# Five token-shift mixes of a recurrent stage on VectorE alone, its 64-row products in pairs, its row norms on ScalarE

## The chip, the cores and the metric

The kernel runs on one core of a Trainium2 chip. It has five engines that run their own instruction streams and meet at semaphores: TensorE (PE in the profile) for matrix products, VectorE (DVE), ScalarE (ACT), GpSimd (POOL) and SyncE (SP), which issues most transfers. The time is device microseconds of one execution of the whole program, as the median of several runs.

## What is computed

The reference is a chain of four blocks over 16 sequences of 128 rows of 512 numbers, in float32: attention over the rows and then over a context with an MLP, a grouped cross attention, a recurrent block, and a latent attention with an MLP. Only the third is touched. It is

```python
xa = _ln(x, ln1_w, ln1_b)
sx = jnp.concatenate([state[:, 1:2] - xa[:, :1], xa[:, :-1] - xa[:, 1:]], axis=1)
xxx = jnp.tanh((xa + sx * maa_x) @ maa_w1).reshape(b, l, 5, DM)
xxx = jnp.einsum('blfd,fde->blfe', xxx, maa_w2)
xm = xa[:, :, None] + sx[:, :, None] * (maa_stack + xxx)
xk, xw, xv, xr, xg = (xm[:, :, j] for j in range(5))
w = jnp.exp(-jnp.exp(time_decay + jnp.tanh(xw @ td_w1) @ td_w2))
# r, k, v = xr @ Wr.T, xk @ Wk.T, xv @ Wv.T;  g = silu(xg @ Wg.T)
def step(s, rkvw):
    a = k_t[..., :, None] * v_t[..., None, :]
    out = jnp.einsum('bhi,bhij->bhj', r_t, u * a + s)
    return a + w_t[..., :, None] * s, out
# out is normed per head, gated by g, projected by Wo, added to x, normed again,
# shifted with the row before and sent through a gated feed-forward layer
```

The five rows of `xm` are the mixes: each is the normed row plus the difference to the row before it, times a factor that comes from a product of rank 32.

## The kernel before

The recurrent stage is `recurrence_phase`. Every engine runs the same pipeline of steps (`run_steps`, line 2142). In one step five sequences are in work at five depths: `ahead` is being loaded and normed, `front` is mixed and projected, `middle` is scanned, `back` is normed by heads and projected, `tail` leaves the feed-forward layer. With 16 sequences there are 20 steps, of which twelve have all five. The order of work inside a step is written out by hand, once for each engine, in that engine's own `step` function, and an engine never goes past an instruction that waits.

- VectorE: for the middle sequence, eight units u of `inputs(u)` (the product of keys and values, line 2665) and `scan(u)` (the decaying sum, line 2677), with everything else put between them. `mix` (line 2651) multiplies a bank of the factor by the row difference `sx_t` into the tile `mixtmp`, one instruction for each of the five mixes, in the order 1, 2, 0, 3, 4. `norm_apply` (line 2630) scales the rows of `ahead` and `back`. `make_gate` (line 2656) and `shift_front` (line 2643, which makes `sx_t`) stand at the end of a step.
- GpSimd: `multiply_states` (line 2396) multiplies each scan's result by the receptance; `add_rows` (line 2389) adds the rows `xa_t` to `mixtmp` into one of two tiles `xm`; `rsqrt` (line 2378) raises a variance to the power -1/2; `bonus_values` is line 2403.
- TensorE: `low_rank` (line 2903) forms the first rank-32 product with features on the partitions, in a piece of 128 rows and one of 32. `mix_pair` (line 2915) and `mix` (line 2930) form the factors with 64-row weights; `mix_pair` alternates two of them, which lie in different halves of the rows. `decay_high` (line 2947) has the same 64-row form. `project`, `keys` (line 2876), `rows` (line 2882) and the transposes (line 2869) follow. `sum_heads` (line 2984) adds up each unit after GpSimd's product.
- ScalarE: `low_rank_tanh` (line 2501, five pieces), `first_states` (line 2466, the first column that a scan needs), `make_decay` (line 2472), `rows_front` (line 2481, scales and shifts the transposed rows into `xa_t`), `gate` (line 2535).

Products go through five PSUM banks, a to d and n. `StepBanks` holds a list of which item uses which bank in what order; TensorE fills a bank (`begin`, `done`), and whoever reads it last gives it back.

## Time and profile before

| | |
|---|---|
| median of three runs | 3513.13 us (3513.01 to 3519.1) |
| profiled execution | 3515.94 us |
| its span, first to last instruction | 3514.2 us |
| mean granted TensorE clock of the span | 0.975 of full speed |
| busy over the span: PE, DVE, ACT, POOL | 3222.5, 1748.5, 1131.0, 900.5 us |

The recurrent stage lies from about 1571 to 2516 us of the span. A step of the steady part is seen best in the order of time of each engine. A row of that view gives the start, the busy time, the engine and line, what is written and read with shapes, how many alike stand in a row, and in brackets how long the engine had stood idle before it and who ended the idleness. A scan has the name `TENSOR_TENSOR_SCAN` in the trace and `SCALAR_TENSOR_TENSOR` in the tables of the order.

### The profile page before, as it was taken

The page shows a single profiled execution, that of the slowest core. Times are in us where ns is not written, and L with a number is a line of the kernel's source. Part 1 is how long each engine was busy: PE and PEld are TensorE (multiplying, and loading weights), DVE is VectorE, ACT ScalarE, POOL GpSimd, SP SyncE. Part 2 cuts the span into 40 slices and gives each one's busy share as a digit, 9 for nine tenths or more (in the row PEclk, how much of TensorE's full clock was granted, in tenths as well). Part 3 has the DMA queues.
Part 4 walks back from the last instruction along what each step waited for, and adds up shares of the span by engine and source line. Part 5 has one row for each costly group of instructions (what it writes and reads, how often), then busy time and mean ns, then how long its engine had stood idle before and what let it go on. Part 6 is the DMA issues. An engine that isn't in the chain of part 4 may idle for free. (4 is left out here: it accounts for less than half of the span.)

```text
span 3514.2 us, 52783 instructions
## 1 busy us (share of the span) xinstructions
PE 3222.5 (92%) x19344; PEld 2128.6 (61%) x19344; DVE 1748.5 (50%) x2503; ACT 1131.0 (32%) x4052; POOL 900.5 (26%) x614
## 2 busy tenths in 40 slices
PE   7999899989999888867899999997799999899999
PEld 5665556557666555546666666664455555466675
DVE  4555556510000378864788888888264454400000
ACT  2444234412111366642232332332133333311111
POOL 2333233300000022223555555565100000100000
PEclk9999999999999899988999999999899999999999
DMA  4110321110000141111011111110130110101010
GB/s 164 43 41 32 119 89 56 34 66 12 24 15 21 40 159 48 44 62 40 26 46 37 36 49 37 36 46 28 60 128 32 33 41 22 49 19 36 21 33 12
DMA packets 104308, 170.19 MB, mean 48 GB/s; under 512 B 16512, under 2 KB 54016, under 8 KB 100736
## 3 DMA queue, kind: packets, MB, share of 16 engines
q1 hardware_dynamic: 99296, 124.58, 11.1%
q10 hardware_dynamic: 4896, 44.04, 3.1%
q8 instruction: 75, 1.23, 0.1%
q14 instruction: 41, 0.34, 0.0%
HBM read 135.03 MB, written 33.55 MB: 48 GB/s over the span
## 5 line engine op out<-in xcount | busy, mean ns | idle before, releaser
L2396 POOL TENSOR_TENSOR rec_S<-rec_S,rec_r_t 128x1024 f32<-128x1024 f32 x128 | 309.8, 2421 | 315.1 <-DVE rec_S L2677 315.1
L2677 DVE TENSOR_TENSOR_SCAN rec_S<-rec_decay,rec_S 128x1024 f32<-128x1024 f32 x128 | 321.9, 2515 | 22.7 <-ACT rec_S L2466 19.4
L2076 PE MATMUL mlp_bank<-mlp_src_t,region_a 128*128 128x256 f32 x1024 | 224.8, 382 | 3.1 <-ACT mlp_src_t L1997 3.1
L2076 PE MATMUL pmlp_bank<-pmlp_src_t,region_a 128*128 128x256 f32 x1024 | 224.9, 382 | 1.9 <-ACT pmlp_src_t L1997 1.9
L2088 PE MATMUL mlp_bank<-region_a,mlp_h_t 128*128 128x512 f32 x512 | 221.1, 592 | 0.0
L2088 PE MATMUL pmlp_bank<-region_a,pmlp_h_t 128*128 128x512 f32 x512 | 221.1, 592 | 0.0
L2076 PEld LDWEIGHTS mlp_bank<-mlp_src_t,region_a 128*128 128x128 f32 x1024 | 196.5, 192 | 33.3 <-issue 6.8
L2076 PEld LDWEIGHTS pmlp_bank<-pmlp_src_t,region_a 128*128 128x128 f32 x1024 | 196.5, 192 | 32.0 <-issue 5.5
L1505 ACT ACTIVATE group_scores<-group_scores,group_negmax 128x128 f32<-128x128 f32 x512 | 197.6, 391 | 28.6 <-DVE group_negmax L1599 18.7
L2043 DVE TENSOR_TENSOR mlp_y<-mlp_bank,mlp_xres 128x512 f32<-128x512 f32 x16 | 11.1, 691 | 375.4 <-PE mlp_bank L2088 375.4
L2043 DVE TENSOR_TENSOR pmlp_y<-pmlp_bank,pmlp_xres 128x512 f32<-128x512 f32 x16 | 11.1, 691 | 364.6 <-PE pmlp_bank L2088 364.6
L2088 PEld LDWEIGHTS mlp_bank<-region_a,mlp_h_t 128*128 128x128 f32 x512 | 96.9, 190 | 118.5 <-issue 118.5
L2088 PEld LDWEIGHTS pmlp_bank<-region_a,pmlp_h_t 128*128 128x128 f32 x512 | 96.9, 190 | 118.5 <-issue 118.5
L2006 ACT ACTIVATE pmlp_h_t<-pmlp_bank,vectors 128x256 f32<-128x256 f32 x128 | 53.7, 470 | 353.8 <-PE pmlp_bank L2076 353.8
L2006 ACT ACTIVATE mlp_h_t<-mlp_bank,vectors 128x256 f32<-128x256 f32 x128 | 53.7, 470 | 348.6 <-PE mlp_bank L2076 348.6
L2665 DVE TENSOR_TENSOR rec_S<-rec_vb,rec_k 128x1016 f32<-128x1016 f32 x128 | 154.0, 1203 | 0.0
L599 ACT ACTIVATE latent_scores<-latent_scores,region_a 128x256 f32<-128x256 f32 x256 | 126.4, 497 | 71.6 <-DVE region_a L789 71.6
L2984 PE MATMUL rec_rec_out<-rec_S,head_sum 128*32 128x256 f32 x1024 | 86.4, 400 | 57.6 <-POOL rec_S L2396 57.6
L973 PE MATMUL latent_pjA<-latent_src_t,F_query_key 128*128 128x512 f32 x256 | 122.0, 602 | 3.3 <-ACT latent_k_t L589 2.3
L599 ACT ACTIVATE self_scores<-self_scores,self_negmax 128x128 f32<-128x128 f32 x256 | 98.8, 391 | 77.1 <-DVE self_negmax L789 77.1
L599 ACT ACTIVATE cross_scores<-cross_scores,cross_negmax 128x128 f32<-128x128 f32 x256 | 98.8, 390 | 76.4 <-DVE cross_negmax L789 76.4
L2389 POOL TENSOR_TENSOR rec_xm<-rec_mixtmp,rec_xa_t 128x512 f32<-128x512 f32 x80 | 106.8, 1335 | 64.2 <-DVE rec_mixtmp L2651 64.2
(363 smaller groups left out, 6496.4 us busy)
## 6 DMA issues: line engine op xcount, KB each, us to landing
rec_vb<-v_by_head SPq DMA_DIRECT2D x32, 512.0 KB, 4.2
region_a<-in_C_w ACTq DMA_DIRECT2D x2, 4096.0 KB, 20.5
region_a<-in_G_w ACTq DMA_DIRECT2D x2, 4096.0 KB, 19.5
self_xres<-in_x SPq DMA_DIRECT2D x16, 256.0 KB, 2.6
rows_A<-self_xres SPq DMA_DIRECT2D x16, 256.0 KB, 2.0
cross_ctx_t<-in_ctx_t SPq DMA_DIRECT2D x16, 256.0 KB, 3.3
cross_xres<-rows_A SPq DMA_DIRECT2D x16, 256.0 KB, 2.6
rows_B<-cross_xres SPq DMA_DIRECT2D x16, 256.0 KB, 2.0
```

What stands on the lines that cost most here:

```text
L599: nc.scalar.activation(S[:, u, at, :], S[:, u, at, :], ACT.Exp, bias=negmax[:, u, at.start // KB:at.start // KB + 1], accum_out=rowsum[:, ...
L973: last = nc.tensor.matmul(pj.bank(item)[:, :], Wk[:, c, n * 128:n * 128 + 128], src_t[:, c, :, :], start=c == 0, stop=c == C - 1)
L1505: nc.scalar.activation(S[:, u, at, :], S[:, u, at, :], ACT.Exp, bias=negmax[:, u, at:at + 1], accum_out=rowsum[:, u // UPS, sum_column(u, ...
L2006: hidden = nc.scalar.activation(h_t[:, 2 * n + i, :], ph.bank(("h", n))[:, i * TT:(i + 1) * TT], ACT.Gelu_apprx_tanh, bias=vec(cfg["b1"], ...
L2043: nc.vector.tensor_tensor(y[:, k, :], po.bank(("out", k))[:, :], xres[:, k, :], ALU.add)\
L2076: product = nc.tensor.matmul(ph.bank(item)[:, i * TT:(i + 1) * TT], W1[:, c, f:f + 128], src_t[:, c, :, :], start=c == 0, stop=c == C - 1)
L2088: product = nc.tensor.matmul(po.bank(item)[:, :], h_t[:, c, k * T:k * T + T], W2[:, c, :], start=c == 0, stop=c == HC - 1)
L2389: nc.gpsimd.tensor_tensor(xm[at % 2][:, :, :], mixtmp[:, :, :], xa_t[:, :, 1:T + 1], ALU.add)\
L2396: nc.gpsimd.tensor_tensor(S[u % 4][:, :, :], S[u % 4][:, :, :], bcast(r_t[:, s.k, UNITS[u][0], :], [128, JH, T], 1), ALU.mult)\
L2665: nc.vector.tensor_tensor(S[u % 4][:, :, 1:T], vb[jh][:, :, 0:T - 1], bcast(k_bank[s.k][:, m * T:m * T + T - 1], [128, JH, T - 1], 1), ALU ...
L2677: nc.vector.tensor_tensor_scan(St[:, :, :].rearrange(flat), decay[m][:, :, :].rearrange(flat), St[:, :, :].rearrange(flat), 0.0, ALU.mult, ...
L2984: last = nc.tensor.matmul(rec_out[32 * g:32 * g + 32, jh * 2 * T:(jh + 1) * 2 * T], head_sum, S[u % 4][:, 2 * g:2 * g + 2, :], start=m == ...
```

## The change

It has four parts, all in the recurrent stage.

1. **The low-rank product** is made with rows on the partitions, all five factors side by side (160 columns). One tanh writes it to `low_rows`, in which a column of ones stands beside each factor. Three transposes bring it to a bank, item `lt`, and ScalarE copies that to the three `low` tiles.
2. **Pairs.** Mixes 1 and 2 lie in one tile now; the decay's second product goes with mix 0 (`decay_and_mix`), mix 3 with mix 4. The halves of output and feed-forward products are split or put together anew around them, and TensorE transposes the rows of `ahead` ahead of the feed-forward keys.
3. **The mixes.** VectorE multiplies in place in the bank, waits for that, and adds the rows from the bank into `xm`. GpSimd's `add_rows` and the tile `mixtmp` are gone. `sx_t` is made from `xa_t` and a copy of it that ScalarE writes back into the bank `x`. `make_gate` moves ahead of the last unit.
4. **The norms.** GpSimd also multiplies the negative mean (formed by VectorE) by the factor, and ScalarE normalises in one instruction with scale and bias.

```diff
-    MIX_TILE = {0: (0, 0), 1: (0, 64), 2: (1, 0), 3: (1, 64), 4: (2, 0)}
+    MIX_TILE = {1: (0, 0), 2: (0, 64), 0: (1, 0), 3: (1, 64), 4: (2, 0)}
...
+        low_rows = sb("low_rows", [128, NMIX, 2 * DM])
-        mixtmp = sb("mixtmp", [128, C, T])
...
-            ("a", "mx", 0), ("b", "mix1", 0), ("a", "mix2", 0), ("n", "mean", 2),
+            ("a", "mx", 0), ("a", "lt", 0), ("b", "mix1", 0), ("a", "mix2", 0), ("n", "mean", 2),
...  GpSimd
+                pool.wait_ge(out_done, n * 2 + 1)
+                nc.gpsimd.tensor_tensor(out[:, 1:2], tile[:, 8:9], out[:, 0:1], ALU.mult).then_inc(out_done, 1)
-            def add_rows(s, f):
-                nc.gpsimd.tensor_tensor(xm[at % 2][:, :, :], mixtmp[:, :, :], xa_t[:, :, 1:T + 1], ALU.add)\
...  ScalarE
+                last.then_inc(first_done, 1)
+                act.wait_ge(first_done, s.n * 3 + 2)
+                nc.scalar.activation(chunks(banks.bank("x")), xa_t[:, :, 1:T + 1], ACT.Copy).then_inc(first_done, 1)
+            def normalise(n, out, rows, scale, scale_done, out_done):
+                act.wait_ge(scale_done, n * 2 + 2)
+                nc.scalar.activation(out[:, :], rows[:, :], ACT.Identity, scale=scale[:, 0:1], bias=scale[:, 1:2])\
+                    .then_inc(out_done, 1)
...
+                nc.scalar.activation(low_rows[:, :, 0:DM],
+                                     banks.bank("mx")[:, 0:NMIX * DM].rearrange("p (f d) -> p f d", f=NMIX), ACT.Tanh)\
+                    .then_inc(banks.free_sem("mx"), 1)
+            def low_rank_copy(s):
+                full(act, s, "lt")
+                for tile in range(3):
+                    p = 128 if tile < 2 else 64
+                    last = nc.scalar.copy(low[tile][0:p, :], banks.bank("lt")[0:p, tile * T:(tile + 1) * T])
+                    last.then_inc(low_done if tile < 2 else banks.free_sem("lt"), 1)
...  VectorE
+                nc.vector.tensor_scalar(tile[:, 8:9], tile[:, 6:7], -1.0, None, ALU.mult)
...
-                nc.vector.tensor_tensor(sx_t[:, :, :], xa_t[:, :, 0:T], xa_t[:, :, 1:T + 1], ALU.subtract)\
-                    .then_inc(sx_done, 1)
+                nc.vector.tensor_tensor(sx_t[:, :, :], xa_t[:, :, 0:T], chunks(banks.bank("x")), ALU.subtract)\
+                    .then_inc(banks.free_sem("x"), 1)
...
-                nc.vector.tensor_tensor(mixtmp[:, :, :], chunks(banks.bank(f"mix{f}")), sx_t[:, :, :], ALU.mult)\
+                bank = chunks(banks.bank(f"mix{f}"))
+                nc.vector.tensor_tensor(bank, bank, sx_t[:, :, :], ALU.mult).then_inc(mixed, 1)
+                dve.wait_ge(mixed, s.n * NMIX + at + 1)
+                nc.vector.tensor_tensor(xm[at % 2][:, :, :], bank, xa_t[:, :, 1:T + 1], ALU.add)\
                     .then_inc(banks.free_sem(f"mix{f}"), 1)
...  TensorE
+                for n, (w, c, t) in enumerate(parts):
+                    last = nc.tensor.matmul(banks.bank("mx")[:, 0:NMIX * DM], xa_t[:, c, t:t + T], w[:, c, :],
+                                            start=n == 0, stop=n == len(parts) - 1)
```

On TensorE the start of a step, from the low-rank product to the first pair, reads before (each row of a matrix product is twice as many passes in the trace):

```order
L2903 MATMUL rec_bank_a<-rec_xa_t,region_a 128x128 x4
L2903 MATMUL rec_bank_a<-rec_xa_t,rec_w_shift 128x128 x4
L2903 MATMUL rec_bank_a<-rec_xa_t,region_a 32x128 x4
L2903 MATMUL rec_bank_a<-rec_xa_t,rec_w_shift 32x128 x4
L2984 MATMUL rec_rec_out<-rec_S,head_sum 32x256 x4
L2915 MATMUL rec_bank_b<-rec_low,region_a 128x128
L2915 MATMUL rec_bank_a<-rec_low,region_a 128x128
```

and now

```order
L2898 MATMUL rec_bank_a<-region_a,rec_xa_t 128x160 x4
L2898 MATMUL rec_bank_a<-rec_w_shift,rec_xa_t 128x160 x4
L2987 MATMUL rec_rec_out<-rec_S,head_sum 32x256 x4
L2906 MATMUL rec_bank_a<-ident,rec_low_rows 128x128 x2
L2906 MATMUL rec_bank_a<-ident,rec_low_rows 64x128
L2880 MATMUL rec_bank_c<-region_a,rec_f_in 128x512
L2913 MATMUL rec_bank_b<-rec_low,region_a 128x128
L2913 MATMUL rec_bank_a<-rec_low,region_a 128x128
```

The four groups of the low-rank product have become two, and the transposes (line 2906) and a quarter of the feed-forward gate stand between it and the pair.

On VectorE, from the first scan of a step to the second mix, before (line 2688 gathers the heads of `back`, line 2692 takes their mean off):

```order
L2677 SCALAR_TENSOR_TENSOR rec_S<-rec_decay,rec_S 128x1024
L2651 TENSOR_TENSOR rec_mixtmp<-rec_bank_b,rec_sx_t 128x512
L2688 TENSOR_TENSOR rec_og<-rec_rec_out,rec_bv 128x512
L2665 TENSOR_TENSOR rec_S<-rec_vb,rec_k 128x8x127
L2692 TENSOR_TENSOR rec_og<-rec_og,rec_bank_n 128x512
L2677 SCALAR_TENSOR_TENSOR rec_S<-rec_decay,rec_S 128x1024
L2651 TENSOR_TENSOR rec_mixtmp<-rec_bank_a,rec_sx_t 128x512
```

and now

```order
L2686 SCALAR_TENSOR_TENSOR rec_S<-rec_decay,rec_S 128x1024
L2652 TENSOR_TENSOR rec_bank_b<-rec_bank_b,rec_sx_t 128x512
L2660 TENSOR_TENSOR rec_xm<-rec_bank_b,rec_xa_t 128x512
L2697 TENSOR_TENSOR rec_og<-rec_rec_out,rec_bv 128x512
L2674 TENSOR_TENSOR rec_S<-rec_vb,rec_k 128x8x127
L2701 TENSOR_TENSOR rec_og<-rec_og,rec_bank_n 128x512
L2686 SCALAR_TENSOR_TENSOR rec_S<-rec_decay,rec_S 128x1024
L2652 TENSOR_TENSOR rec_bank_a<-rec_bank_a,rec_sx_t 128x512
L2660 TENSOR_TENSOR rec_xm<-rec_bank_a,rec_xa_t 128x512
```

Behind each multiplication an addition stands. At the end of the step, from the scan of unit 6 on, VectorE had

```order
L2677 SCALAR_TENSOR_TENSOR rec_S<-rec_decay,rec_S 128x1024
L2630 TENSOR_SCALAR rec_x<-rec_x,rec_stats,rec_rstd 128x512
L2745 SCALAR_TENSOR_TENSOR rec_f_in<-rec_bank_c,rec_w_same,rec_f_in 128x128 x4
L2665 TENSOR_TENSOR rec_S<-rec_vb,rec_k 128x8x127
L2677 SCALAR_TENSOR_TENSOR rec_S<-rec_decay,rec_S 128x1024
L2643 TENSOR_TENSOR rec_sx_t<-rec_xa_t 128x512
L2656 SCALAR_TENSOR_TENSOR rec_g<-rec_g,rec_bank_a 128x512
```

and has

```order
L2686 SCALAR_TENSOR_TENSOR rec_S<-rec_decay,rec_S 128x1024
L2750 SCALAR_TENSOR_TENSOR rec_f_in<-rec_bank_c,rec_w_same,rec_f_in 128x128 x4
L2665 SCALAR_TENSOR_TENSOR rec_g<-rec_g,rec_bank_a 128x512
L2674 TENSOR_TENSOR rec_S<-rec_vb,rec_k 128x8x127
L2686 SCALAR_TENSOR_TENSOR rec_S<-rec_decay,rec_S 128x1024
L2642 TENSOR_TENSOR rec_sx_t<-rec_xa_t,rec_bank_b 128x512
```

The normalisation of `ahead` is gone and the gate (line 2656, now 2665) stands ahead of the last unit.

ScalarE has, from the receptance's copy to the first column of the last unit, before

```order
L2466 COPY rec_S<-rec_s 128x8
L2519 ACTIVATE rec_r_t<-rec_bank_d 128x512
L2492 ACTIVATE rec_f_in<-rec_bank_c,vectors,rec_w_shift 128x127 x8
L2466 COPY rec_S<-rec_s 128x8
L2472 ACTIVATE rec_decay<-rec_e_t 128x8x127
L2541 COPY rec_c_sb<-rec_bank_b 128x128
L2478 COPY rec_xa_t<-rec_st 128x4
L2481 ACTIVATE rec_xa_t<-rec_bank_b,vectors 128x128 x4
L2466 COPY rec_S<-rec_s 128x8
```

and now

```order
L2472 ACTIVATE rec_y<-rec_x,rec_rstd 128x512
L2520 ACTIVATE rec_r_t<-rec_bank_d 128x512
L2489 ACTIVATE rec_f_in<-rec_bank_c,vectors,rec_w_shift 128x127 x8
L2446 COPY rec_S<-rec_s 128x8
L2452 ACTIVATE rec_decay<-rec_e_t 128x8x127
L2472 ACTIVATE rec_x<-rec_x,rec_rstd 128x512
L2536 ACTIVATE rec_g<-rec_bank_a 128x512
L2542 COPY rec_c_sb<-rec_bank_b 128x128
L2460 COPY rec_xa_t<-rec_st 128x4
L2463 ACTIVATE rec_xa_t<-rec_bank_b,vectors 128x128 x4
L2468 ACTIVATE rec_bank_b<-rec_xa_t 128x512
L2446 COPY rec_S<-rec_s 128x8
```

The two normalisations (line 2472), the gate's tanh (line 2536, which stood near the end of the step) and the copy back into the bank (line 2468) have been put into that stretch.

## Rows read from the trace of the kernel before

**Rows 1.** Windows, steady steps: stretch, its us, then the engines' busy us.
```profile
1750.00:2300.00 550.00, 503.60 (x3769) 377.28 (x3767) 474.65 (x614) 174.66 (x470) 311.20 (x195) 1.00 0.13 40
```

**Rows 2.** Waits, 1750 to 2300 us: who waited for whom: us, times, longest.
```profile
DVE rec_mixtmp L2651 <- PE rec_bank_b L2915: 32.5, 10, 3.3
```

**Rows 3.** Timeline of VectorE, one steady step: start us, us, instruction [idle before].
```profile
1990.87 2.29 DVE L2677 TENSOR_TENSOR_SCAN rec_S<-rec_decay,rec_S 128x1024 f32<-128x1024 f32 x1 [1.36 <-ACT rec_S L2466]
...
1995.60 2.52 DVE L2677 TENSOR_TENSOR_SCAN rec_S<-rec_decay,rec_S 128x1024 f32<-128x1024 f32 x1
2001.45 0.69 DVE L2651 TENSOR_TENSOR rec_mixtmp<-rec_bank_b,rec_sx_t 128x512 f32<-128x512 f32 x1 [3.34 <-PE rec_bank_b L2915]
...
2004.72 2.28 DVE L2677 TENSOR_TENSOR_SCAN rec_S<-rec_decay,rec_S 128x1024 f32<-128x1024 f32 x1
...
2008.62 0.19 DVE L2699 TENSOR_SCALAR rec_hv<-rec_bank_n 128x32 f32<-128x32 f32 x1 [1.04 <-PE rec_bank_n L3000]
...
2012.94 2.28 DVE L2677 TENSOR_TENSOR_SCAN rec_S<-rec_decay,rec_S 128x1024 f32<-128x1024 f32 x1
...
2017.64 3.31 DVE L2677 TENSOR_TENSOR_SCAN rec_S<-rec_decay,rec_S 128x1024 f32<-128x1024 f32 x1
...
2022.00 0.69 DVE L2753 SCALAR_TENSOR_TENSOR rec_bank_d<-rec_y,rec_bank_d 128x512 f32<-128x512 f32 x1
2022.72 0.69 DVE L2755 SCALAR_TENSOR_TENSOR rec_y<-rec_bank_d,rec_x 128x512 f32<-128x512 f32 x1
2023.33 1.20 DVE L2665 TENSOR_TENSOR rec_S<-rec_vb,rec_k 128x1016 f32<-128x1016 f32 x1
...
2026.34 2.29 DVE L2677 TENSOR_TENSOR_SCAN rec_S<-rec_decay,rec_S 128x1024 f32<-128x1024 f32 x1
...
2030.46 1.12 DVE L2630 TENSOR_SCALAR rec_y<-rec_x,rec_stats,rec_rstd 128x512 f32<-128x512 f32 x1
2031.50 3.27 DVE L2677 TENSOR_TENSOR_SCAN rec_S<-rec_decay,rec_S 128x1024 f32<-128x1024 f32 x1
...
2038.51 2.28 DVE L2677 TENSOR_TENSOR_SCAN rec_S<-rec_decay,rec_S 128x1024 f32<-128x1024 f32 x1
2040.71 0.52 DVE L2630 TENSOR_SCALAR rec_x<-rec_x,rec_stats,rec_rstd 128x512 f32<-128x512 f32 x1
...
2044.73 2.29 DVE L2677 TENSOR_TENSOR_SCAN rec_S<-rec_decay,rec_S 128x1024 f32<-128x1024 f32 x1 [1.35 <-ACT rec_S L2466]
```

**Rows 4.** The same timeline of GpSimd.
```profile
1993.24 2.73 POOL L2396 TENSOR_TENSOR rec_S<-rec_S,rec_r_t 128x1024 f32<-128x1024 f32 x1 [2.44 <-DVE rec_S L2677]
...
2015.30 2.36 POOL L2396 TENSOR_TENSOR rec_S<-rec_S,rec_r_t 128x1024 f32<-128x1024 f32 x1 [4.04 <-DVE rec_S L2677]
2017.63 1.17 POOL L2389 TENSOR_TENSOR rec_xm<-rec_mixtmp,rec_xa_t 128x512 f32<-128x512 f32 x1
...
2043.42 1.27 POOL L2403 TENSOR_TENSOR rec_bv<-rec_v_t,rec_c_sb 128x512 f32<-128x512 f32 x1
```

**Rows 5.** The same timeline of TensorE.
```profile
1994.58 1.15 PE L2903 MATMUL rec_bank_a<-rec_xa_t,region_a 128*128 128x128 f32 x8 [1.17 <-DVE rec_g L2656]
...
2000.11 0.34 PE L2915 MATMUL rec_bank_b<-rec_low,region_a 64*128 64x128 f32 x1 [1.18 <-ACT rec_low L2501]
...
2010.32 0.64 PE L2984 MATMUL rec_rec_out<-rec_S,head_sum 128*32 128x256 f32 x8
...
2012.23 1.16 PE L2930 MATMUL rec_bank_a<-rec_low,region_a 64*128 64x128 f32 x8
```

**Rows 6.** The same timeline of ScalarE.
```profile
1998.53 1.43 ACT L2501 ACTIVATE rec_low<-rec_bank_a 32x128 f32<-32x128 f32 x5 [4.06 <-PE rec_bank_a L2903]
...
2043.04 1.50 ACT L2481 ACTIVATE rec_xa_t<-rec_bank_b,vectors 128x128 f32<-128x128 f32 x4 [1.85 <-PE rec_bank_b L2869]
```

**Rows 7.** Timeline of all engines where the stage begins.
```profile
1572.20 1.15 DVE L2835 MEMSET rec_low<- 1x128 f32 x5
...
1578.71 2.08 PE L2903 MATMUL rec_bank_a<-rec_xa_t,region_a 128*128 128x128 f32 x8 [1.59 <-ACT rec_xa_t L2481]
```

237 lines of the change are left out of this document (104 added, 133 removed).

## The prediction

> **What bounds the kernel now.** I read the windows of the stage first, then the waits, then the order of time on each engine in one steady step, because every edit lies in the recurrent stage, and most of its time is one repeated step. In 550 us of steady steps TensorE is busy for 503.60 and VectorE for 474.65 at a full granted clock [rows 1]. A step lasts 53.86 us: from the last scan at 1990.87 to the last scan of the next step at 2044.73 [rows 3]. So TensorE works 49.3 us of a step and VectorE 46.5, and neither is the bound alone: each waits for the other in turn. The waits name the largest place: VectorE's first mix waits for TensorE's product 32.5 us in ten steps [rows 2]. In the step itself TensorE's low-rank product waits 1.17 for VectorE's gate [rows 5], and the last scan 1.35 for ScalarE's first columns [rows 3].
>
> VectorE never skips ahead, so I take it as the ruler. A step is eight scans of 2.28 us, which nothing shortens, and eight gaps between them. A gap is the end of one scan to the end of the next, less 2.28. From the nine scans [rows 3], gap 7-0 (from the last scan of a step to the first of the next) is 2.68, then 0-1: 6.60, 1-2: 5.94, 2-3: 3.45, 3-4: 5.40, 4-5: 3.86, 5-6: 3.74, 6-7: 3.95. Sum 35.6, with 18.2 of scans 53.8. The forecast is these eight gaps again.
>
> **What a scan does while GpSimd works.** The scans at 2017.64 and 2031.50 last 3.31 and 3.27 instead of 2.28 [rows 3]. At 2017.63 GpSimd had just begun an addition of 1.17, a hundredth of a microsecond before the scan [rows 4]. The scan ends 2.15 after that addition, so it ran from about 0.13 before GpSimd's recorded end. In the other order, the scan at 1990.87 ends at 1993.16 and the product starts at 1993.24 [rows 3, 4]. I take it that a scan and a GpSimd operation exclude each other. This speaks for taking the additions off GpSimd and also sets floors below, since GpSimd's product of a scan (2.36 at 2015.30) starts 0.08 after it: a gap can't be under 0.08 + 2.36 - 0.13 = 2.31. The product at 1993.24 lasts 2.73 [rows 4], beside the shift, which reads two tensors of SBUF; the shift now reads one in a bank, so I take 2.36 there too.
>
> **What the change adds to VectorE.** Five additions of a step, 128x512, one input in PSUM. The nearest row is the pair at 2022.00 and 2022.72, the same shapes, the first in place in a bank, the second dependent on it: 0.69 each, pitch 0.72 inside the pair and 0.61 after it [rows 3]. A mix now takes one pitch of 0.61 and will take 0.72 + 0.61, so 0.72 more, 3.6 a step. Two small negations of the mean: between 0.07 (the operation overlaps) and 0.2 each; I take 0.1, because they wait for nothing of their own, 0.2 a step. Leaving: the two normalisations, 1.12 at 2030.46 and 0.52 at 2040.71 [rows 3], with a pitch of 1.04 (to the scan at 2031.50) and about 0.43, so 1.5. The gate moves from after the last scan to before it at no change in work. VectorE's own work grows by 2.3 us, to 48.8, less what the two scans lose to additions, 2 x 1.03, so 46.7.
>
> The Trainium skill (VectorE: DVE Perf Modes, the section "The DRAIN you can't avoid") says that a semaphore between two VectorE operations costs nothing extra. The rows show 0.11 more inside the dependent pair (0.72 against 0.61). By the page the additions would cost 5 x 0.11 = 0.55 a step less; I go by the row, and the page's case is rival 3.
>
> **What leaves TensorE.** The low-rank product was four groups of eight passes of 128 columns, the first 1.15 long at 1994.58, 3.75 in all (the tanh behind the fourth starts at 1998.53 [rows 6]); it becomes 16 passes of 160 columns, an estimate of 16 x 0.123 x 160/128 = 2.4 from the pitch of that row [rows 5]. Added are three transposes, 0.4. Four 64-row products (decay, mixes 0, 3 and 4) run one by one, 1.16 each as mix 0 at 2012.23; they become two pairs, and a pair, like the one that starts at 2000.11 and whose first mix VectorE takes 1.34 later, occupies TensorE some 1.1 [rows 3, 5]. That saves 2 x 1.1. TensorE's work falls by 1.35 + 2.2 - 0.4 = 3.1, to 46.2 a step.
>
> **ScalarE** gains two normalisations of 128x512 (the nearest row is the four quarter ones with scale and bias at 2043.04, 1.50 together [rows 6]: no more than 1.5, no less than one of them, 0.4; 0.7 taken, since one instruction has one start), a copy of the rows into the bank (0.6) and three low-rank copies (0.85), and loses four of five tanh (1.43 at 1998.53 becomes 0.3). It works 174.66 of 550 us [rows 1], so 17 a step; the 1.7 more costs only where somebody waits, which is the first columns of the last unit. SyncE issues the same transfers in the same order; only the count one of them waits for is renamed.
>
> **Now the gaps.** T is the moment the first scan of a step can run (1995.84 before, 2.28 ahead of its end).
> Gap 7-0: the gate no longer fills it, so shift, inputs and the scan would be ready after 1.86; GpSimd's floor decides, 2.30. It was 2.68 with the longer product.
> Gap 0-1: TensorE no longer waits for the gate (1.17 [rows 5]) and is through with the 2.4 of low-rank at about T - 0.8. It then stands before the last head sum, whose product GpSimd ends at T + 0.13 (1995.97 before [rows 4]). Head sum 0.6 (0.64 at 2010.32 [rows 5]), transposes 0.5, the three copies 0.85 (all three, since the second mix reuses their bank), handovers 0.25, and from the pair's start to the mix 1.34 (2000.11 to 2001.45 [rows 3, 5]): T + 3.65 against T + 5.6 before. VectorE's wait there falls from 3.34 to 1.4. The gap is that, the addition, gather, inputs, centre and 0.15 of waiting for the mean: 5.2, from 6.60.
> Gap 1-2: the addition fills most of the 1.04 at 2008.62 [rows 3]; 0.2 remains, and 0.15 for the transposed factor, as the pair of decay and mix 0 reaches TensorE late: 5.9.
> Gap 2-3: one addition more, and the 1.03 of exclusion gone: 3.15, from 3.45.
> Gap 3-4: addition 0.72, negation 0.1, wait for the pair of mixes 3 and 4 about 0.35: 6.0, from 5.40. TensorE gets to that pair about when the scan ends, since it has the value product and half of the output rows ahead of it.
> Gap 4-5: the factor's power waits for the scan, takes 0.35 after it, its second operation 0.4 more, then GpSimd's product: it ends 3.1 after the scan, so the scan can run after 3.0, from 3.86.
> Gap 5-6: 3.85, from 3.74 (one negation).
> Gap 6-7: ScalarE's first columns come earlier, since TensorE transposes the rows ahead of the feed-forward keys; but GpSimd's bonus product (1.27 at 2043.42 [rows 4]) now ends 3.7 after the scan and excludes the next one: 3.55, from 3.95.
> Sum 32.95, with 18.25 of scans **51.2 us a step, 2.6 less**. The two sides of it: adding 2.3 of own work, and taking away 2.1 of exclusion and 2.8 of waiting.
>
> Twelve steps have all five roles and one is nearly such: 13 x 2.6 = 34. In the filling the memsets (five took 1.15 [rows 7]) shrink by 1, the low-rank product runs at half the speed (2.08 for eight passes against 1.15 [rows 5, 7]) and saves 2, one unpaired product less saves 1, and each first mix skips the hop to GpSimd; two further half-full steps are TensorE's and gain some 3 between them. With 2 for the step before the draining: 10 in all. The drain has no mixes and loses about 0.5 (a longer factor and normalisation). 34 + 10 - 0.5 = 44. Against the profiled execution's 3515.9 that is 3472; the median of before lies 2.8 lower, at 3513.1, so **3469**.
>
> **Rivals.** (1) The waits come back in part. TensorE still works 46.2 of 51.2 and is held at four places in my walk: before the last head sum, the mean, the value product (whose bank ScalarE's exponentials free) and the fifth head sum. If each costs VectorE another 0.3, a step gains 1.4: 13 x 1.4 + 5 = 23, **3490**. For it: TensorE would still be busy nine tenths of the step, as now [rows 1], and each of the four holds is of some engine that it feeds itself. Against: the floors of gaps 7-0, 4-5 and 6-7 are GpSimd's, which has less to do.
> (2) Slower. The first mix is the place: low-rank, head sum, transposes and copies are a chain of five handovers in place of three. If TensorE comes to it as late as now (T - 1.26), the first mix is ready at T + 5.8; the five additions then are all uncovered, and the sum of the gaps is 2.68 + 7.3 + 6.5 + 3.5 + 6.1 + 3.5 + 3.9 + 3.95 = 37.4, 1.8 a step more: 14 x 1.8 = 25, **3538**. It decides when the gaps sum to over 35.6, which needs the first mix 2 us later than I have it and no gain elsewhere. Against it are the 1.17 that TensorE stands idle before the low-rank product and the 3.1 it loses of work.
> (3) The dependent pair costs no more than an independent one, by the page above: 13 x 0.55 = 7 more gained, **3462**.
> (4) VectorE's added work just eats what it waited: **3513**, no change.
>
> **How the numbers follow.** Forecast 0.55, rival 1 0.18, rival 3 0.08, rival 4 0.07, rival 2 0.12. The range 3450 to 3502 holds the first three, and takes in the bounds of ScalarE's normalisations and the negations. Runs of this kernel can tell about 0.2%, 7 us, from no change. Faster by more: 0.81; within: 0.07; slower: 0.12.
>
> **What would show it.** In the trace of after, a steady step of 51.2 from last scan to last scan; no scan over 2.9 in gaps 2-3; the wait for the first mix near 1.4; pitch of 0.72 inside a mix; TensorE busy 46 a step. It is wrong if the first mix still waits 3 us, if scans grow in gaps 4-5 or 7-0 beyond 2.8, or if ScalarE's first columns hold the last scan.

## The result: 3458.9 us, and the profile after

The changed kernel takes 3458.89 us in the median (3457.59 to 3460.93), the kernel before 3514.97 in the same comparison: a ratio of 0.9839, with a 95% interval of 0.9822 to 0.9857. The forecast was 3469 in a range of 3450 to 3502. Sign and range held, and the account of the steady step held in its main lines; the gain is 56 us where 44 were forecast, and the section on the prediction says where the other 12 came from.

In the windows view the steady stretch of [rows 1] now reads as follows (kernel after; stretch, its us, busy us of TensorE, its weight loads, VectorE, ScalarE, GpSimd, then granted clock):

```profile
1750.00:2300.00 550.00, 502.04 (x3867) 365.36 (x3865) 519.24 (x707) 208.91 (x529) 259.00 (x175) 1.00 0.14 42
```

It holds 10.9 steps of 50.6 us in place of 10.2 of 53.8. VectorE is now busy for 47.8 us of a step, TensorE for 46.2. The waits view of the kernel after, same stretch, answers to [rows 2]:

```profile
DVE rec_bank_b L2652 <- PE rec_bank_b L2913: 13.5, 22, 1.1
```

The row counts 22 waits in eleven steps: the one in front of the first mix, 1.0 each, and one of 0.20 in front of the fourth, which uses the same bank. [Rows 2] has the first mix alone, 32.5 us in ten steps. So of the 3.34 in front of the first mix 1.01 is left. The timeline of VectorE in a steady step of the kernel after answers to [rows 3]:

```profile
1995.03 0.68 DVE L2652 TENSOR_TENSOR rec_bank_a<-rec_bank_a,rec_sx_t 128x512 f32<-128x512 f32 x1
1995.74 0.69 DVE L2660 TENSOR_TENSOR rec_xm<-rec_bank_a,rec_xa_t 128x512 f32<-128x512 f32 x1
...
1997.58 2.60 DVE L2686 TENSOR_TENSOR_SCAN rec_S<-rec_decay,rec_S 128x1024 f32<-128x1024 f32 x1
...
2003.96 2.28 DVE L2686 TENSOR_TENSOR_SCAN rec_S<-rec_decay,rec_S 128x1024 f32<-128x1024 f32 x1
...
2009.01 3.06 DVE L2686 TENSOR_TENSOR_SCAN rec_S<-rec_decay,rec_S 128x1024 f32<-128x1024 f32 x1
...
2013.90 2.76 DVE L2686 TENSOR_TENSOR_SCAN rec_S<-rec_decay,rec_S 128x1024 f32<-128x1024 f32 x1
2017.67 0.70 DVE L2652 TENSOR_TENSOR rec_bank_b<-rec_bank_b,rec_sx_t 128x512 f32<-128x512 f32 x1 [1.01 <-PE rec_bank_b L2913]
2018.40 0.69 DVE L2660 TENSOR_TENSOR rec_xm<-rec_bank_b,rec_xa_t 128x512 f32<-128x512 f32 x1
2019.01 0.68 DVE L2697 TENSOR_TENSOR rec_og<-rec_rec_out,rec_bv 128x512 f32<-128x512 f32 x1
...
2025.51 0.19 DVE L2708 TENSOR_SCALAR rec_hv<-rec_bank_n 128x32 f32<-128x32 f32 x1 [0.30 <-PE rec_bank_n L3003]
```

The scans at 1997.58, 2009.01 and 2013.90 are units 5, 7 and 0 and still last longer than 2.28. Each starts into a GpSimd operation, as GpSimd's timeline of the same step shows (answering to [rows 4]):

```profile
1992.95 2.50 POOL L2378 TENSOR_TENSOR rec_rstd<-rec_stats,minus_half 128x1 f32<-128x1 f32 x1 [3.58 <-DVE rec_stats L2634]
1995.53 0.19 POOL L2380 TENSOR_TENSOR rec_rstd<-rec_stats,rec_rstd 128x1 f32<-128x1 f32 x1
1995.67 2.37 POOL L2386 TENSOR_TENSOR rec_S<-rec_S,rec_r_t 128x1024 f32<-128x1024 f32 x1
...
2008.65 1.27 POOL L2393 TENSOR_TENSOR rec_bv<-rec_v_t,rec_c_sb 128x512 f32<-128x512 f32 x1
2012.15 2.36 POOL L2386 TENSOR_TENSOR rec_S<-rec_S,rec_r_t 128x1024 f32<-128x1024 f32 x1 [2.23 <-DVE rec_S L2686]
```

TensorE and ScalarE at the head of a step, kernel after, answer to [rows 5, 6]: the low-rank product in two groups, one tanh, the wait for GpSimd's product ahead of the head sum, three transposes, three copies.

```profile
2011.48 1.25 PE L2898 MATMUL rec_bank_a<-region_a,rec_xa_t 128*128 128x160 f32 x8
2012.57 1.25 PE L2898 MATMUL rec_bank_a<-rec_w_shift,rec_xa_t 128*128 128x160 f32 x8
2013.85 0.30 ACT L2495 ACTIVATE rec_low_rows<-rec_bank_a 128x160 f32<-128x160 f32 x1 [2.27 <-PE rec_bank_a L2898]
2014.57 0.64 PE L2987 MATMUL rec_rec_out<-rec_S,head_sum 128*32 128x256 f32 x8 [0.75 <-POOL rec_S L2386]
2015.13 0.55 PE L2906 MATMUL rec_bank_a<-ident,rec_low_rows 128*128 128x128 f32 x3
...
2015.72 0.58 ACT L2503 COPY rec_low<-rec_bank_a 128x128 f32<-128x128 f32 x3 [1.56 <-PE rec_bank_a L2906]
```

**Where the 58 us of the two traces went.** End of scan to end of scan: up to the last scan of the first sequence 10.0 us, the next step 5.9, the twelve full steps 37.8 (3.15 each), the two draining ones 1.8 and 2.3. Half a microsecond of the first 10.0 lies ahead of the stage: VectorE's first memset of the `low` or `low_rows` tiles, my mark for its beginning, starts at 1571.67 before and at 1571.13 after. (In the traces of all kernels it starts between 1569.7 and 1575.4, though nothing ahead of it was changed; below I count the filling from there.)

The table gives a typical steady step of every kernel by its gaps, as the prediction defines them (end of one scan to the end of the next, less 2.28), from the starts and lengths of the scans in the traces. Each step is their sum and 18.24. In the kernels before and after the twelve full steps differ by 0.3 us at most; e1_adds, e4_tensor_only, e2_gpadds and e3_dvenorms have longer steps among them, which the table leaves out and the text comes to.

| kernel | 7-0 | 0-1 | 1-2 | 2-3 | 3-4 | 4-5 | 5-6 | 6-7 | sum | median, us | ratio to before |
|---|---|---|---|---|---|---|---|---|---|---|---|
| before | 2.68 | 6.60 | 5.94 | 3.45 | 5.40 | 3.86 | 3.74 | 3.95 | 35.6 | 3515.0 | 1 |
| forecast | 2.30 | 5.2 | 5.9 | 3.15 | 6.0 | 3.0 | 3.85 | 3.55 | 32.95 | 3469 | |
| after | 2.31 | 4.95 | 5.95 | 3.17 | 5.89 | 2.79 | 3.78 | 3.55 | 32.4 | 3458.9 | 0.9839 |
| e1_adds | 2.68 | 6.99 | 5.94 | 3.24 | 6.34 | 2.87 | 4.71 | 3.76 | 36.5 | 3542.6 | 1.0070 |
| e4_tensor_only | 2.31 | 5.09 | 5.94 | 3.46 | 4.84 | 3.86 | 3.74 | 3.76 | 33.0 | 3473.4 | 0.9875 |
| e2_gpadds | 2.32 | 5.21 | 5.95 | 3.45 | 4.84 | 2.79 | 3.79 | 4.58 | 32.9 | 3471.7 | 0.9867 |
| e3_dvenorms | 2.33 | 5.71 | 5.95 | 3.17 | 5.88 | 2.87 | 3.74 | 3.76 | 33.4 | 3479.1 | 0.9891 |
| e5_unpaired | 2.32 | 4.88 | 5.94 | 3.17 | 5.90 | 2.78 | 3.78 | 3.57 | 32.3 | 3465.6 | 0.9853 |
| e9_gate | 3.28 | 5.11 | 5.94 | 3.17 | 5.89 | 2.78 | 3.79 | 2.32 | 32.3 | 3463.7 | 0.9850 |
| e12_late_unpaired | 3.26 | 5.12 | 5.94 | 3.16 | 5.89 | 2.79 | 3.79 | 2.32 | 32.3 | 3470.2 | 0.9865 |
| e6_half | 1.84 | 4.69 | 5.95 | 3.17 | 5.89 | 2.48 | 3.79 | 2.78 | 30.6 | 3428.7 | 0.9748 |
| e7_bonus | 2.32 | 4.89 | 5.95 | 3.17 | 5.89 | 2.79 | 3.78 | 2.78 | 31.6 | 3451.9 | 0.9807 |
| e8_residual | 2.30 | 4.89 | 5.95 | 3.17 | 6.17 | 2.47 | 3.79 | 3.56 | 32.3 | 3460.5 | 0.9842 |
| e13_bonus_residual | 2.31 | 4.89 | 5.95 | 3.17 | 6.17 | 2.47 | 3.79 | 2.77 | 31.5 | 3450.5 | 0.9807 |
| e10_both | 2.31 | 4.07 | 5.45 | 3.16 | 6.17 | 2.48 | 3.78 | 3.54 | 31.0 | 3448.4 | 0.9801 |

The half width of each ratio's interval is 0.0016 to 0.0020, some 6 us. The kernel before had medians of 3517.8, 3517.3 and 3518.0 in the three comparisons of the experiments, and the kernel after was measured beside one of 3515.0. Between the kernel after and an experiment the times therefore don't tell single microseconds; where I give such differences they rest on the traces.

### The profile page after: what moved, and what is told of

It reads as the page before. It is cut to its first block and busy times, and to the rows that moved or that the text cites. A ratio compares the mean times of both kernels' runs of the same rounds, so it can differ in the third digit from the quotient of the medians.

```text
span 3455.8 us, 52394 instructions
## 1 busy us (share of the span) xinstructions
PE 3175.1 (92%) x19136; PEld 2078.5 (60%) x19136; DVE 1776.9 (51%) x2577; ACT 1160.8 (34%) x4083; POOL 793.3 (23%) x565
## 5 line engine op out<-in xcount | busy, mean ns | idle before, releaser
L2386 POOL TENSOR_TENSOR rec_S<-rec_S,rec_r_t 128x1024 f32<-128x1024 f32 x128 | 302.0, 2359 | 362.4 <-DVE rec_S L2686 362.3
L2076 PEld LDWEIGHTS mlp_bank<-mlp_src_t,region_a 128*128 128x128 f32 x1024 | 196.2, 192 | 32.9 <-issue 6.8
L1979 POOL TENSOR_TENSOR mlp_xres<-mlp_x,rows 128x512 f32<-128x512 f32 x16 | 20.2, 1264 | 341.0 <-DVE mlp_y L2043 329.6
```

What stands on the lines that cost most here:

```text
L1979: nc.gpsimd.tensor_tensor(xres[:, k, :], xr[:, k, :], row(cfg["b2"]), ALU.add)\
L2076: product = nc.tensor.matmul(ph.bank(item)[:, i * TT:(i + 1) * TT], W1[:, c, f:f + 128], src_t[:, c, :, :], start=c == 0, stop=c == C - 1)
L2386: nc.gpsimd.tensor_tensor(S[u % 4][:, :, :], S[u % 4][:, :, :], bcast(r_t[:, s.k, UNITS[u][0], :], [128, JH, T], 1), ALU.mult)\
```

## Experiments: which part carries the gain

The theory: the parts act by what they take from VectorE's gaps, and the additions on VectorE cost 0.72 each where nothing waits, so that by themselves they lose. The rival: the parts are worth the sum of what each is worth alone. Four kernels take the change apart.

**e1_adds**: the kernel before with the additions moved to VectorE, nothing else.

```diff
-                nc.vector.tensor_tensor(mixtmp[:, :, :], chunks(banks.bank(f"mix{f}")), sx_t[:, :, :], ALU.mult)\
+                nc.vector.tensor_tensor(bank, bank, sx_t[:, :, :], ALU.mult).then_inc(mixed, 1)
...
+                nc.vector.tensor_tensor(xm[at % 2][:, :, :], bank, xa_t[:, :, 1:T + 1], ALU.add)\
...
-                    add_rows(front, 1)
```

> The kernel before with one part alone: VectorE multiplies each mix in place in the bank and adds the rows itself; GpSimd's additions are gone. The gap account (VectorE's eight gaps between scans, own work plus waits plus exclusion with GpSimd): gap 0-1 7.3, 1-2 5.95 (the wait for the variance absorbs the addition), 2-3 3.15 (no exclusion), 3-4 6.4, 4-5 3.5, 5-6 3.75, 6-7 3.95, 7-0 2.68: 54.9 a step, about 3532 us, 1.005 of before. Rival, the exclusion pays for the additions: scans of 3.3 go to 2.3 and nothing is given back, 52.8 a step, about 3500. Rival, TensorE's work alone sets the step: unchanged, 3515.

Measured 3542.56: the part of the change that its name speaks of makes the kernel 0.7% slower. The timeline of VectorE in e1_adds shows why: the wait for the first mix is all but as long as before (3.06 against 3.34), because what it waits for is TensorE.

```profile
1846.54 0.70 DVE L2631 TENSOR_TENSOR rec_bank_b<-rec_bank_b,rec_sx_t 128x512 f32<-128x512 f32 x1 [3.06 <-PE rec_bank_b L2903]
...
1898.33 1.21 DVE L2653 TENSOR_TENSOR rec_S<-rec_vb,rec_k 128x1016 f32<-128x1016 f32 x1 [3.83 <-issue]
```

The gap sum grows by 0.9, for which 13 steps give 12 us. The second row is something else: at each of the four jumps back of the hardware loop (five iterations of two steps) VectorE stands 3.5 to 4.0 us idle before its first instruction behind the branch, with no engine to wait for. Two of the steps behind these are as long, 56.4 us against 54.8, and in both TensorE's granted clock was at its lower level for a while (0.50 from 1952 to 1955 in the first of them, after TensorE had stood idle for 1.85). Together the six steps are 9 us longer than ordinary ones. That makes up most of the difference to the 3532 expected.

**e4_tensor_only**, **e2_gpadds** and **e3_dvenorms** are the changed kernel with both the additions and the norms put back, with the additions back on GpSimd, and with the norms back on VectorE.

```diff
+                nc.gpsimd.tensor_tensor(xm[at % 2][:, :, :], mixtmp[:, :, :], xa_t[:, :, 1:T + 1], ALU.add)\
...
+                nc.vector.tensor_scalar(out[:, :], rows[:, :], tile[:, 6:7], scale[:, 0:1],
+                                        ALU.subtract, ALU.mult).then_inc(out_done, 1)
...
-                nc.scalar.activation(out[:, :], rows[:, :], ACT.Identity, scale=scale[:, 0:1], bias=scale[:, 1:2])\
```

> The kernel after with its third and fourth parts undone: only the low-rank product by rows with its transposes, the pairs, TensorE's new order, the gate's earlier place and the copy into the bank for the shift stay. Gap account: 51.0 to 51.3 a step, about 3466 us (0.986), so that these parts of TensorE's bring 2.5 of the 3.2 us of a step. Rival, the parts need each other, and alone TensorE's bring only the 1.2 that it waited for the gate: 52.6, about 3485.

> The kernel after with its third part undone: VectorE multiplies into the tile mixtmp and GpSimd adds the rows, as before; pairs, low-rank product by rows and ScalarE's norms stay. Gap account: VectorE has 3.6 less to do, of which waits for TensorE take back most, and the additions hold one scan: gaps 4.3, 5.8, 3.5, 5.4, 2.8, 4.1, 3.55, 2.3, a step of 50.0 against 50.6 of after, about 3451 us (0.982 of before). So the additions on VectorE would be the one part that loses. Rival, GpSimd's additions in the way of scans are what the change gained by: 52.6 a step, about 3485.

> The kernel after with its fourth part undone: VectorE normalises the rows of ahead and back, GpSimd only raises the power. Gap account: gap 4-5 from 2.79 to 3.6, gap 6-7 from 3.55 to 3.8, less 0.1 in the two gaps with a negation: 51.5 a step, about 3472 us (0.988). Rival, VectorE's waits absorb the 1.5 us: 50.6, 3459, no difference from after.

Against some 3518 for before, TensorE's parts alone (with the gate's place and the rows' copy in the bank) give 44 us. The norms on top give 2 more, which is within the noise, the additions on top of TensorE's parts cost 6, and both together give some 14 (12 by the ratios). So the parts don't add up: additions and norms are worth something only together. The ordinary steps say the same: 51.3 in e4_tensor_only, 51.2 with the norms, 51.7 with the additions, 50.6 with both.

But ordinary steps are only about half of what both together give. In each of the three kernels some of the twelve full steps are 1 to 2 us longer, 7 to 8 us in all, and in each of these or just ahead of it TensorE's granted clock was at its lower level (1.2 in place of 2.4 GHz) for a while. Such a stretch in e3_dvenorms, then the same place of the next step, by the windows view, and by the timeline of TensorE the 32 passes that were caught in it:

```profile
1862.00:1865.00 3.00, 3.00 (x16) 3.00 (x16) 2.57 (x3) 2.82 (x7) 2.28 (x2) 0.50 0.00 0
1915.00:1918.00 3.00, 3.00 (x29) 3.00 (x29) 2.57 (x4) 2.97 (x7) 2.57 (x2) 1.00 0.00 0
```

```profile
1861.44 5.37 PE L2872 MATMUL rec_bank_d<-rec_f_in,region_a 128*128 128x128 f32 x32
...
1914.72 3.74 PE L2872 MATMUL rec_bank_d<-rec_f_in,region_a 128*128 128x128 f32 x32
```

In the kernels before and after the clock is 1.00 in all twelve full steps. So what additions and norms give together is some 8 us of shorter ordinary steps and some 7 us of steps that no longer lose clock. In e3_dvenorms and e4_tensor_only the stretches begin behind an idle time of TensorE of 2.36 us, which stands in every step (0.38 in the kernel after); why the clock fell in some steps and not in others the runs don't show. The 3466 and 3472 that I had expected for e4_tensor_only and e3_dvenorms leave these steps out, and both are missed by 7.

Two places show what happens in the ordinary steps. In e2_gpadds GpSimd keeps the additions and the norms' factor stands behind one of them (timeline of GpSimd and ScalarE, and the last scan):

```profile
2065.49 3.17 POOL L2392 TENSOR_TENSOR rec_xm<-rec_mixtmp,rec_xa_t 128x512 f32<-128x512 f32 x1
...
2071.57 2.16 POOL L2381 TENSOR_TENSOR rec_rstd<-rec_stats,rec_rstd 128x1 f32<-128x1 f32 x1
...
2073.76 0.81 ACT L2493 ACTIVATE rec_x<-rec_x,rec_rstd 128x512 f32<-128x512 f32 x1 [2.90 <-POOL rec_rstd L2381]
...
2078.32 2.29 DVE L2697 TENSOR_TENSOR_SCAN rec_S<-rec_decay,rec_S 128x1024 f32<-128x1024 f32 x1 [1.42 <-ACT rec_S L2469]
```

An addition started into scan 5 and lasted 3.17 instead of 1.17. The product behind it and the norm's factor came later, the factor was caught by scan 6 (2.16 instead of 0.19), ScalarE normalised late, and the last scan waited 1.42 for the first columns: the 4.58 of gap 6-7. I had said 3451 and taken no such chain into account, a miss of 21 us, of which 8 are the steps that lost clock; the time lies between that and the rival's 3485. In e3_dvenorms TensorE, which now transposes the next rows ahead of the feed-forward keys, stands idle for VectorE's normalisation of them, as it does in e4_tensor_only (2.36). It comes late to the first mix, for which VectorE waits 1.83 in an ordinary step against 1.01 in the kernel after, and the addition behind that mix is uncovered. The rows are TensorE's transposes and VectorE's first mix in e3_dvenorms:

```profile
1914.24 0.65 PE L2865 MATMUL rec_bank_b<-ident,rec_x 128*128 128x128 f32 x4 [2.36 <-DVE rec_x L2619]
...
1926.15 0.70 DVE L2645 TENSOR_TENSOR rec_bank_b<-rec_bank_b,rec_sx_t 128x512 f32<-128x512 f32 x1 [1.83 <-PE rec_bank_b L2911]
```

**e5_unpaired, e9_gate, e12_late_unpaired**: which of TensorE's parts is it? The changed kernel with its 64-row products one at a time, with the gate at the end of the step, and with both. The gate that moves is VectorE's (`make_gate`), as the edit shows; TensorE's and ScalarE's order is that of the kernel after. The expectation of e9_gate, which speaks of TensorE's gate products, describes its edit wrongly.

```diff
-                    mix_pair(front, 3, 4)
+                    mix_one(front, 3)
...
-                if front:
-                    make_gate(front)
                 if middle:
                     inputs(middle, 7)
                     scan(middle, 7)
                 if ahead:
                     shift_front(ahead)
+                if front:
+                    make_gate(front)
```

> The changed kernel with its 64-row products one at a time again: decay_high by itself, mix 0 behind the normalise products, mix 3 by itself, mix 4 behind the keys. The sum of the mix stays in the bank, ScalarE keeps the norms and the gate its place. A pair takes about 1.16 us by the trace of the kernel before and a product by itself as long, so TensorE has two products' time, 2.2 to 2.3 us, more to do in a step of 50.6 us, of which it waits some 4.4 us. Theory A, scans and the VectorE operations between them set the step and TensorE's waits take the two products up: only the first scan of a step, which stands behind the decay factors, comes later, 0.2 us a step, about 3462 us, with TensorE's busy time up and its waits down. Theory B, TensorE's own work sets the step: 2.2 us in each of 14 steps, about 3490 us.

> The changed kernel with TensorE's gate products put back to the end of the step, behind the first of the two low-rank groups' transposes, where they stood before. Theory A, the gate's place carries part of the gain: the low-rank product at the head of the next step waits for the gate's 1.3 us, the decay factors and with them the first scan of the step come later: 1.3 to 1.45 us a step in 14 steps, about 3480 us. Theory B, the gate is short beside TensorE's idle time and its place costs nothing: about 3459 us, within 0.2% of the changed kernel.

> The changed kernel with both parts undone that cost nothing in a steady step when undone alone: the four 64-row products one at a time and the gate at the end of the step. What stays of TensorE's parts is the low-rank product in rows (16 passes of 160 columns, one tanh, three transposes) and the split output rows. Theory A, the two aren't substitutes, and the low-rank form carries the gain in a steady step: 50.6 us a step as in the changed kernel, the first steps longer as in either run alone, about 3470 us. Theory B, each of the two lives on the time that the other leaves TensorE, and only both together cost: 52 us a step or more, 3485 to 3495 us.

In a steady step neither costs anything: the sums are 32.3 in all three. Without the pairs TensorE is busy 525.09 us of the 550 instead of 502.04 and VectorE as before; the 2.2 us a step go into TensorE's own waits. What the two parts are worth, 7, 5 and 11 us by the medians, lies in the filling: from the beginning of the stage to the end of the second sequence's scans these kernels take 4.6, 5.7 and 11.8 us longer than the kernel after (the second sequence's step alone is 53.9, 52.3 and 54.9 us long against 51.4). So in the steady step what is left of TensorE's parts that can carry the gain is the low-rank product in rows, the split output rows, the transposes of the rows of `ahead` in front of the feed-forward keys, and the copy of the rows in the bank; these four I didn't separate.

For the gate I had expected 3480. Its place does decide when the low-rank product starts, but the late gate also changed which engine held which. GpSimd's timeline in e9_gate:

```profile
2011.59 2.38 POOL L2386 TENSOR_TENSOR rec_S<-rec_S,rec_r_t 128x1024 f32<-128x1024 f32 x1 [2.94 <-DVE rec_S L2686]
2013.91 3.28 POOL L2393 TENSOR_TENSOR rec_bv<-rec_v_t,rec_c_sb 128x512 f32<-128x512 f32 x1
```

Scan 7 starts at 2013.68, before the bonus product instead of into it, so the scan is short (2.44 instead of 3.06) and the product long (3.28 instead of 1.27). Gap 6-7 falls by 1.23 and gap 7-0 grows by 0.97. The low-rank product waits 0.52 for the gate (at 2017.43), and 0.2 of that reaches gap 0-1 (5.11 against 4.9).

## Experiments: do a scan and GpSimd exclude each other?

The prediction assumed so from two long scans. The rival: long scans have a cause of their own. **e6_half** halves GpSimd's product (and leaves half of it out), **e7_bonus** moves the bonus product.

```diff
-                nc.gpsimd.tensor_tensor(S[u % 4][:, :, :], S[u % 4][:, :, :],
+                nc.gpsimd.tensor_tensor(S[u % 4][:, 0:JH // 2, :], S[u % 4][:, 0:JH // 2, :],
```

```diff
+                if back and middle:
+                    pool.wait_ge(scan_done, middle.n * NU + 1)
+                if back:
+                    bonus_values(back)
                 if middle:
                     multiply_states(middle, 0)
...
-                    bonus_values(middle)
```

> The changed kernel with GpSimd's product of the state with r on the first half of each unit's channels only; the second half of each unit's product is left out, so the heads' sums are formed from unfinished values. GpSimd's operation falls from about 2.4 us to about 1.2 us; nothing else changes. Theory A, a scan and a GpSimd product can't run beside each other, so a scan that starts into a product waits for it: the gap in front of the first scan falls from 2.30 to about 1.86 us, in front of scan 5 from 2.79 to about 2.55, in front of scan 7 from 3.55 to about 2.9, and the 1.0 us that the second mix waits for TensorE goes: about 48.3 us a step instead of 50.6, about 3427 us. Theory B, the long scans (2.6, 2.8 and 3.1 us instead of 2.28) have a cause of their own: step and time unchanged within 0.2%, about 3459 us.

> The changed kernel with GpSimd's bonus product (v by c, 128x512, 1.27 us) moved from the gap in front of scan 7, which it lengthens from 2.28 to 3.06 us, to the next step behind scan 0. Theory A, that overlap is all that the place costs: the gap in front of scan 7 falls from 3.55 to about 2.95 us, 0.6 us a step, about 3450 us. Theory B, given back: the product of GpSimd on unit 0 starts 1.3 us later, and with it the heads' sum on TensorE in the next stretch, which sets when the second mix is there (VectorE waits 1.0 us for it now): about 3459 us or up to 5 us more.

In e6_half all scans of the steady steps are short again. Its groups by line, VectorE, 1780 to 2250 us:

```profile
L2686 DVE TENSOR_TENSOR_SCAN rec_S<-rec_decay,rec_S 128x1024 f32<-128x1024 f32 x77 | 176.2, 2289 | 3.0
```

77 scans of 2289 ns in the mean, with VectorE's own instructions untouched: the length came from GpSimd. Gaps 7-0, 4-5 and 6-7 fell to 1.84, 2.48 and 2.78, against 1.86, 2.55 and 2.9 expected. Only the wait for the first mix stayed, 1.0 us, where I had expected it to go: the product came earlier, but so did the scan. The floors are confirmed by the gaps. That the time came out right as well, 3428.67 against 3427 expected, is in part luck: a steady step is 48.9 and not 48.3, some 7 us in twelve, and the filling and the draining, for which I had counted two steps' worth, gave more. e7_bonus took 0.77 from gap 6-7 and gave nothing back in the steady step; of the 9 us of twelve steps the filling took 3 again.

A rule of the Trainium skill fits. Its page SBUF — State Buffer, section "Who interferes with whom", says that a VectorE instruction with two SBUF inputs contends with a GpSimd instruction that reads SBUF, that the lock is exclusive, and that the order of issue decides who blocks. Both orders are here: scan 7 is held by the bonus product in the kernel after (3.06), the bonus product by scan 7 in e9_gate (3.28). The multiplications and additions of a mix have one input in a bank, and they are no longer beside GpSimd's operations than alone: the additions of e6_half last 0.69 in both places (43 beside one, 12 alone), the multiplications of the kernel before 0.66 to 0.69 beside one and 0.69 alone. In the kernel after the addition at 1995.74 lies inside the product of 1995.67.

## Experiments: a version that beats both

**e8_residual** makes the residual and its statistics before unit 4's inputs, so that GpSimd's power is done when scan 4 starts. **e10_both** also gathers the heads ahead of the first mix, into its wait. **e13_bonus_residual** joins e8_residual to e7_bonus.

```diff
-                if front:
-                    mix(front, 1)
                 if back:
                     gather(back)
+                if front:
+                    mix(front, 1)
...
-                if middle:
-                    inputs(middle, 4)
                 if back:
                     residual(back)
                 if middle:
+                    inputs(middle, 4)
                     scan(middle, 4)
```

> The changed kernel with VectorE's residual and its statistics ahead of the inputs of unit 4 in place of behind them, so that GpSimd can finish the power before scan 4 starts. Theory A, the 2.50 us that the power lasts (0.5 by itself) and the late product behind it are the scan's doing: power about 0.5 us long, the gap in front of scan 5 falls from 2.79 to about 2.55 us, 3456 us. Theory B, the residual then waits for TensorE's output rows and the gap in front of scan 4 grows by as much: 3459 us or more.

> The same as the run before it, and VectorE gathers the heads' output ahead of its second mix, where it now waits 1.0 us for TensorE in the gap between scans 0 and 1. Theory A, the 0.6 us of the gather fill that wait: 0.6 us a step less from the gap behind the first scan, with the 0.24 of the residual 0.9 in all, about 3447 us. Theory B, the gather itself waits for the head sum, which TensorE makes just ahead of the mix, and the order brings nothing or delays the mix: 3456 us or more.

> The changed kernel with GpSimd's bonus product behind scan 0 of the next step (which by itself took 0.77 us from a step) and the residual ahead of the inputs of unit 4. Theory A, the two places are independent, both being overlaps of a scan with GpSimd: 0.77 + 0.24 = 1.0 us a step less than the changed kernel, 49.6, about 3447 us. Theory B, the earlier product of one is held by the other: no better than the first alone, about 3452 us.

In e8_residual the power is short and free of the scan. GpSimd's timeline:

```profile
2040.85 0.54 POOL L2378 TENSOR_TENSOR rec_rstd<-rec_stats,minus_half 128x1 f32<-128x1 f32 x1 [2.68 <-DVE rec_stats L2634]
2041.47 0.19 POOL L2380 TENSOR_TENSOR rec_rstd<-rec_stats,rec_rstd 128x1 f32<-128x1 f32 x1
```

Gap 4-5 falls by 0.3 as theory A says, and gap 3-4 grows by as much: the inputs (1.24 to the scan) now stand directly before the scan that needs them, where small statistics stood, and the residual starts 0.83 behind the operation ahead of it. That is theory B's result, but hardly by its cause: TensorE's last output rows ended at 2037.81, 1.0 us before the residual starts. What holds the residual for its 0.2 I didn't find out. e13_bonus_residual accordingly is no better than e7_bonus (3450.5 and 3451.9, steps of 49.8 in both); the 3447 of its theory A did not come. e10_both gives more than expected in a step, 1.4 us (timeline of VectorE):

```profile
2013.86 0.66 DVE L2697 TENSOR_TENSOR rec_og<-rec_rec_out,rec_bv 128x512 f32<-128x512 f32 x1
2014.95 0.70 DVE L2652 TENSOR_TENSOR rec_bank_b<-rec_bank_b,rec_sx_t 128x512 f32<-128x512 f32 x1 [0.43 <-PE rec_bank_b L2912]
```

The wait falls from 1.01 to 0.43, and since TensorE's means and variances start earlier too, gap 0-1 loses its 0.2 of waiting for the mean and gap 1-2 its 0.3 for the variance and 0.2 more. The first scan comes 5.5 us later (1619.01 against 1613.49), but 4.2 of that lie ahead of the stage, where nothing was changed; 1.3 are the stage's. e10_both has the lowest median of the kernels with all the work, 3448.38 us: 0.9801 (0.9785 to 0.9817) of before, clear of the kernel after (0.9822 to 0.9857) but not of e7_bonus and e13_bonus_residual.

## The prediction, point by point

- **The ruler of eight gaps: right.** No gap was off by more than 0.3, and 50.6 us a step stand against 51.2. Four came out shorter than forecast (by 0.25, 0.11, 0.21 and 0.07), none longer by more than 0.05, and twelve steps make 7 us of that. It was also right that neither engine's busy time is the step: 23 us more work for TensorE in the 550 us of e5_unpaired moved no gap.
- **The additions: right.** 0.71 to 0.73 inside a pair and 0.61 after it (2017.67, 2018.40, 2019.01). Rival 3 falls: the sentence of the Trainium skill's VectorE: DVE Perf Modes, "The DRAIN you can't avoid", that the semaphore costs nothing extra, doesn't hold for these dependent pairs (whether the wait or the dependence takes the 0.11, the runs don't separate). The time landed nearer to that rival's 3462 than to my 3469, but for other reasons.
- **Exclusion and waiting: the split was wrong.** I had a step lose 2.1 of exclusion and 2.8 of waiting, and VectorE busy for 46.7. It is busy for 47.8. What the scans last beyond 2.28 fell from 2.26 (0.24, 1.03 and 0.99) to 1.58 only (0.32, 0.78 and 0.48), so 0.7, because the scans of gaps 7-0 and 6-7 are held longer now and that of 4-5 still is; my gaps had these holds in them, the sum of the busy time had not. VectorE's idle time fell from 7.4 to 2.8 a step, 4.6. So what pays for the additions is waiting taken away, and little of it exclusion.
- **Gap 0-1: mechanism right, 0.25 to 0.3 too long.** The mix comes 3.29 after T (2017.67 against 2014.38), not 3.65. The term is the three copies, 0.58 and not 0.85. My reason that TensorE would no longer wait for the gate was of no weight: the head sum waits for GpSimd's product anyway (0.75 at 2014.57), and e9_gate lets it wait for the gate again at 0.2 in that gap.
- **Gap 4-5: mechanism right, 0.2 too long.** From the power's end to the product's start, with the factor's second operation between them, it is 0.22 and not 0.4 (1995.45 to 1995.67). The power was held by the scan as said: 2.50 long.
- **The pairs: sized right, counted wrongly.** TensorE lost its 2.2 us, and the steady step would be the same without that: e5_unpaired has the same gaps.
- **The filling: mis-sized.** I had 8 us for it, and 2.6 for the second sequence's step, the "nearly such" one of the thirteen; together 10.6. They gave 15.9: 10.0 to the end of the first sequence (0.5 of it ahead of the stage) and 5.9 in the next step. TensorE's work counts for more there: the products that e5_unpaired puts back, which move no gap of a steady step, make this step 2.5 us longer (53.9 against 51.4), and the granted clock is 0.85. The windows of that next step, kernel before and then kernel after:

```profile
1667.00:1724.00 57.00, 49.77 (x357) 40.16 (x357) 42.95 (x58) 15.44 (x44) 31.85 (x19) 0.85 0.09 27
```

```profile
1657.00:1708.00 51.00, 45.08 (x336) 35.26 (x336) 46.08 (x63) 18.85 (x48) 23.87 (x16) 0.85 0.11 33
```

  TensorE's 4.7 us less are four fifths of the 5.9, if all of them count. That they do isn't shown: TensorE is idle for 7.2 us of this step before and for 5.9 after.
- **The draining: wrong in sign.** I had it lose 0.5; the last sequence's step became 2.3 shorter (47.5 to 45.2). Its longest wait is VectorE's for TensorE's output rows, in the gap in front of scan 4: 2.75 us before, 0.73 after. The change splits the output rows anew; whether that is the cause I didn't test. With the 7 of the twelve steps and the 5 of the filling these 3 make up what the forecast lacks against the two traces (58 us).
- **The normalisation on ScalarE**: 0.82 (at 1995.75) where I took 0.7. Nobody waited for its rows; TensorE's transposes wait 0.38 (at 2004.93) for a small copy that stands behind it on ScalarE, and the last scan no longer waits for first columns.
- **Rivals 1, 2 and 4** did not come. But rival 2's place, additions that stand uncovered because the first mix is late, is what e1_adds shows: 3542.6, where the chain to the first mix is not shortened.
